# Softmax denominators of the first half's queries: probabilities added on VectorE, one multiplication by ones on TensorE

## What is computed

```python
paths = jax.nn.sigmoid(x @ Wp + bp)             # (8, 1024, 8 heads, 5)
agree = pq * pk + (1.0 - pq) * (1.0 - pk)
sim = jnp.cumprod(agree, axis=-1).sum(axis=-1) / DEPTH
sim = jnp.where(mask[None, None], -jnp.inf, sim)   # causal
attn = jax.nn.softmax(sim, axis=-1)
ctx = jnp.einsum('bhqk,bhkd->bhqd', attn, V)
x = _layernorm(x + ctx @ Wo)
x = _layernorm(x + w_down(silu(w_gate(x)) * w_up(x)))
```

## Time and profile before

| | |
|---|---|
| median of 3 runs | 944.2 us (944.07 to 945.45) |
| profiled execution | 944.54 us, of which 942.8 us from the first to the last instruction |
| TensorE matmul busy | 846.7 us (90%) |
| VectorE busy | 480.6 us (51%) |
| ScalarE busy | 456.3 us (48%) |
| GpSimd busy | 227.6 us (24%) |
| mean granted TensorE clock | 0.973 of full speed |

### The profile page before, as it was taken

One profiled execution on the slowest core, in us unless ns is written; L12 is line 12 of the kernel. 1 busy time (PEld: TensorE's weight loads), 2 busy tenths in 40 slices (PEclk: granted clock), 3 DMA queues, 4 the chain that ended last, 5 costly groups with the idle time before them and its releaser, 6 DMA issues.

```text
span 942.8 us, 15453 instructions
## 1 busy us (share of the span) xinstructions
PE 846.7 (90%) x6146; PEld 412.6 (44%) x6146; DVE 480.6 (51%) x1021; ACT 456.3 (48%) x721; POOL 227.6 (24%) x266
## 2 busy tenths in 40 slices
PE   5399998899989999799988999899998999898984
PEld 3144355443544436344454435444363444344352
DVE  2844436445465436554275354654355552754375
ACT  2255644546355454554546454555535545364431
POOL 0021231223222232131321223122421313222222
PEclk9599999999999999999999999999999999999997
DMA  6841443140421424104431314214150043200001
GB/s 214 208 105 46 90 90 113 45 88 26 112 90 46 113 45 113 67 23 112 91 112 46 71 43 112 90 46 90 49 132 23 24 113 83 75 2 22 1 1 47
DMA packets 44362, 71.09 MB, mean 75 GB/s; under 512 B 3584, under 2 KB 21248, under 8 KB 44288
## 3 DMA queue, kind: packets, MB, share of 16 engines
q1 hardware_dynamic: 44288, 70.07, 28.4%
HBM read 53.28 MB, written 16.78 MB: 74 GB/s over the span
## 4 chain that ended last, share of the span: by engine, by line
PE 73%; DVE 9%; ACT 8%; issue 3%; DMA 3%; POOL 3%; SPq 1%; POOLq 0%; ACTq 0%; DVEq 0%
PE ctx_ps L788 14%; PE misc L823 12%; PE den_ps L788 12%; PE slot L766 11%; PE misc L833 8%; PE misc L742 7%; ACT probs L451 6%; PE misc L800 6%; POOL work L404 2%; DVE work L612 2%; PE misc L751 2%; DVE x L595 2%; DVE ctx_raw L522 1%; DMA phi_dram<-phi_lo 1%; ACT work L463 1%
## 5 line engine op out<-in xcount | busy, mean ns | idle before, releaser
L451 ACT ACTIVATE probs<-slot 128x1024 f32<-128x1024 f32 (+3 forms) x384 | 290.4, 808 | 374.5 <-PE slot L766 374.2
L766 PE MATMUL slot<-query_stack,key_stack 128*128 128x512 f16 (+3 forms) x768 | 162.8, 334 | 16.6 <-DMA query_stack<-phi_dram 15.4
L788 PE MATMUL ctx_ps<-probs,vz_sb 128*32 128x512 f32 (+3 forms) x1536 | 166.0, 504 | 10.0 <-DVE ctx_raw L522 9.7
L404 POOL TENSOR_TENSOR work<-work 128x512 f16<-128x512 f32 x96 | 112.7, 1174 | 216.5 <-ACT work L469 216.5
L788 PE MATMUL den_ps<-probs,ones 128*32 128x512 f32 (+3 forms) x1536 | 163.0, 496 | 0.0
L390 POOL TENSOR_SCALAR_AFFINE_SELECT probs<-probs 128x512 f32<-128x512 f32 x128 | 81.7, 640 | 309.2 <-ACT probs L451 308.1
L612 DVE SCALAR_TENSOR_TENSOR work<-work,misc 128x512 f32<-128x512 f32 x90 | 61.8, 686 | 165.7 <-ACT work L463 165.7
L823 PE MATMUL misc<-x1T_hi,w_parts 128*128 128x512 f16 x360 | 136.7, 380 | 1.4 <-DVE x1T_lo L602 0.9
L823 PE MATMUL misc<-x1T_lo,w_parts 128*128 128x512 f16 x360 | 136.4, 379 | 0.0
L766 PEld LDWEIGHTS slot<-query_stack,key_stack 128*128 128x128 f16 x768 | 56.9, 98 | 171.2 <-issue 121.7
L833 PE MATMUL misc<-w_parts,work 128*128 128x256 bf16 x720 | 83.7, 273 | 8.3 <-POOL work L404 8.3
(11 more groups left out here) (74 smaller groups left out, 645.3 us busy)
## 6 DMA issues: line engine op xcount, KB each, us to landing
key_stack<-phi_dram SPq DMA_DIRECT2D x64, 256.0 KB, 6.0
query_stack<-phi_dram SPq DMA_DIRECT2D x64, 256.0 KB, 6.6
xT_sb<-in_xT_dram SPq DMA_DIRECT2D x8, 1024.0 KB, 5.1
x_sb<-in_x_dram SPq DMA_DIRECT2D x8, 1024.0 KB, 5.5
out_dram<-x SPq DMA_DIRECT2D x15, 512.0 KB, 2.9
phi_dram<-phi_hi SPq DMA_DIRECT2D x16, 256.0 KB, 2.1
phi_dram<-phi_lo SPq DMA_DIRECT2D x16, 256.0 KB, 2.3
work<-in_wgT_dram SPq DMA_DIRECT2D x1, 768.0 KB, 8.1
```

Source lines behind the costliest of these rows:

```text
L404: pool.tensor_tensor(hid_lo[:, n % M1, :], hid[:, n % HSLOTS, :], hid_hi[:, n % M1, :], ALU.subtract).then_inc(hid_lo_ready, 1)
L451: act.activation(probs[:, s % P_SLOTS, 2 * p:2 * p + 2, off:CH], slot[p][:, :, off:CH], ACT.Exp).then_inc(slot_drained[p], 1)
L766: mm = pe.matmul(slot[p][:, k, off:CH], key_stack[:, h, P * j:P * (j + 1)], query_stack[:, h, CH * c + off:CH * (c + 1)], start=True, stop ...
L788: mm = pe.matmul(sums[32 * k:32 * k + 32, off:CH], w, probs[:, s % P_SLOTS, k, off:CH], start=first, stop=final)
```

## The change

In the short chunks (c=0) the multiplication by ones no longer runs in every step. VectorE gets a new entry `sum` in the list (`add_up`), one step after `exps` and ahead of that step's other work: at j=1 it copies the first 128 columns of step j=0's probabilities into a new tile `acc` and adds the other 384 columns of the two steps; at j=2 and j=3 it adds 256 and 128 columns, for the four heads in one instruction each. In the chunk's last step TensorE multiplies `acc` by ones once, 512 columns wide. ScalarE's `exps`, before it overwrites a slot of `probs` that held a short step, now waits for the sum that read it (for j=0, the sum at j=1) besides `weigh`. `normalise` waits for the multiplication of `acc`. Steps of the second half (c=1) keep their multiplications.

```diff
+    SHORT = [i for i, (q, c, g, j) in enumerate(STEPS) if c == 0]
...
+        if s >= 1 and (s - 1) % NS in SHORT:
+            plan += [("sum", *divmod(s - 1, NS))]
         plan += between(b, i)
...
+        acc = sb("acc", [P, 4, CH], F32)
...
                     act.wait_ge(pv_done, s - P_SLOTS + 1)
+                    b2, i2 = divmod(s - P_SLOTS, NS)
+                    if i2 in SHORT:
+
+                        act.wait_ge(summed, SUMMED[b2, i2 + (STEPS[i2][3] == 0)])
...
+            def add_up(b, i):
+
+                q, c, g, j = STEPS[i]
+                if j == 0:
+                    return
+                s = NS * b + i
+                own = probs[:, s % P_SLOTS, :, P * j:CH]
+                dve.wait_ge(masked, len(DIAG) * b + DIAG.index(i) + 1)
+                if j == 1:
+                    if NG * b + g >= 1:
+                        dve.wait_ge(acc_used, NG * b + g)
+                    first = probs[:, (s - 1) % P_SLOTS, :, :]
+                    dve.tensor_copy(acc[:, :, 0:P], first[:, :, 0:P]).then_inc(summed, 1)
+                    dve.tensor_tensor(acc[:, :, P:CH], first[:, :, P:CH], own, ALU.add).then_inc(summed, 1)
+                else:
+                    dve.wait_ge(summed, SUMMED[b, i] - 1)
+                    dve.tensor_tensor(acc[:, :, P * j:CH], acc[:, :, P * j:CH], own, ALU.add).then_inc(summed, 1)
...
                 dve.wait_ge(pv_done, NS * b + LAST[q] + 1)
+                if c == 0:
+                    dve.wait_ge(acc_used, NG * b + g + 1)
...
-                for sums, taken in ((ctx_ps, ctx_out), (den_ps, den_out)):
-                    if first and NQ * b + q >= 1:
-                        pe.wait_ge(taken, NQ * b + q)
+                if first and NQ * b + q >= 1:
+                    pe.wait_ge(ctx_out, NQ * b + q)
+                for k in range(4):
+                    h = 4 * g + k
+                    mm = pe.matmul(ctx_ps[32 * k:32 * k + 32, off:CH], vz_sb[:, b % 2, j, 32 * h:32 * h + 32],
+                                   probs[:, s % P_SLOTS, k, off:CH], start=first, stop=final)
+                if c == 0:
+
+                    mm.then_inc(pv_done, 1)
+                    if final:
+                        pe.wait_ge(summed, SUMMED[b, i])
+                        if NQ * b + q >= 1:
+                            pe.wait_ge(den_out, NQ * b + q)
+                        for k in range(4):
+                            mm = pe.matmul(den_ps[32 * k:32 * k + 32, :], ones[:, :], acc[:, k, :],
+                                           start=True, stop=True)
+                        mm.then_inc(acc_used, 1)
+                else:
+                    if first:
+                        pe.wait_ge(den_out, NQ * b + q)
                     for k in range(4):
-                        h = 4 * g + k
-                        w = vz_sb[:, b % 2, j, 32 * h:32 * h + 32] if taken is ctx_out else ones[:, :]
-                        mm = pe.matmul(sums[32 * k:32 * k + 32, off:CH], w,
+                        mm = pe.matmul(den_ps[32 * k:32 * k + 32, off:CH], ones[:, :],
                                        probs[:, s % P_SLOTS, k, off:CH], start=first, stop=final)
-                mm.then_inc(pv_done, 1)
+                    mm.then_inc(pv_done, 1)
```

More of the change, by code:

```diff
@@ L180, in seq_postln_kernel @@
             turn += 1
+    SUMMED, pieces = {}, 0
+    for b in range(B):
+        for i in SHORT:
+            pieces += (0, 2, 1, 1)[STEPS[i][3]]
+            SUMMED[b, i] = pieces
     NORM = {tuple(n): at for at, n in enumerate([n for what, *n in PLAN if what == "stats"])}
@@ L275, in seq_postln_kernel @@
         den_out = sem("den_out")
+        summed = sem("summed")
+        acc_used = sem("acc_used")
         den_recip_ready = sem("den_recip_ready")
@@ L697, in _ @@
                     split_weights()
+                elif what == "sum":
+                    add_up(*n)
                 elif what == "normalise":
```

## The result

The changed kernel takes 968.94 us (median of 4 runs, 968.58 to 971.09) against 944.48 us for the kernel before beside it: ratio 1.0238, 95% interval 1.0189 to 1.0287, so 24.5 us slower. The forecast was 961, the range 948 to 974.

The account below looks back on a forecast made before the run. TensorE (90% busy) bound the kernel, with half-idle VectorE nearly as tight in steps 2 to 7 and the bound in step 6. Middle batches +6, batch 0 +6.5, batch 7 +4 on 944.54 gave 961 us, range 948 to 974.

Parts of the forecast that it names:

- The adds: VectorE, each short chunk: copy 0.42 us, adds 1.75, 1.2 and 0.65 us; 4 us a chunk, 64 us in 16 chunks.
- its idle time: TensorE ahead of `turn_f`, step 6 of middle batches: grows from 2.48 to 4.8 us, `turn_f` moving from 271.42 to 272.9.
- batch 0's scores: Scores of step 4 in batch 0: wait for the first copy and add, moving from 54.87 to 58.7, +3.8 us.
- The net of a middle batch at full clock: Middle batches, TensorE savings against VectorE delays with no fall of the clock: +0.9 us a batch.
- that wait, named as a sign: Step 8 of middle batches: gate matmul newly waits for the VectorE instruction behind the second add, 1.3 us late.
- All three terms of the sum: Whole run: middle batches +6 us, batch 0 +6.5 and batch 7 +4, together 16.5 us.
- the last one: Batch 7, with no next batch's work to cover VectorE: +4 us, bounds +1 and +6.
- With idle times twice as long I take a fall of that length in all six: Middle batches, step 6: the clock falls for about 3.3 us in all six, before in three; +6 us in all.
- with one of twice the length some +13: Upper bound for the six middle batches together if the clock's fall lasts twice as long: some +13 us.
- TensorE stays the bound: Rival, whole run: every add lies in VectorE's idle half, the 21 us come in full, 923 us; chance 0.07.
- the 21 us: TensorE's saving from fewer multiplications by ones: 1.32 us a short chunk, 21 us in 16 chunks.
- Dearer adds: Rival: VectorE and GpSimd in each other's way, 0.3 us more per add on the chain, 973 us; chance 0.13.

Follow-up runs that it names:

- experiment 3: Changed kernel plus 20 unread 512-column matmuls in TensorE's step 6 idle time, batches 1 to 6: 957.96 us, ratio 1.0134 to the kernel before.
- experiment 5: Changed kernel with the new way for the first short chunk of a batch alone, the second multiplied by ones every step: 950.2 us, ratio 1.0042.
- experiment 6: Changed kernel with the new way for the second short chunk of a batch alone, the first multiplied by ones every step: 962.61 us, ratio 1.016.
- experiment 2: Changed kernel with adds and copies cut to one column (denominators not computed) and ten unread matmuls in step 6: 937.06 us, ratio 0.9904.
- experiment 8: Changed kernel with second chunk's adds moved behind `x1_low` and the hidden products, second half of weights' split later, 10 unread matmuls: 959.32 us, ratio 1.0125.
- experiment 4: Kernel before the change plus 10 unread 512-column matmuls in step 6 idle time of batches 1 to 6: 940.06 us, ratio 0.9934.
- experiment 10: Changed kernel, new way in batches 1 to 6 alone, adds behind what TensorE waits for, four `probs` slots, 10 unread matmuls: 930.33 us, ratio 0.9836.

## Why the prediction was right, and where its sizes were off

**Right, step by step.** The adds took what was derived: copy 0.42, adds 1.75, 1.21 and 0.69 us (the row that the first was taken from the earlier trace rows reads int32, but the times agree). `turn_f` came at 281.10 - 8.17 = 272.93 (forecast 272.9), its idle time at 4.73 (4.8); batch 0's scores at 58.45 (58.7). The net of a middle batch at full clock, +0.9, was measured as 110.98 - 110.07 = 0.91 (experiment 3), with the wait for L648 that it derives. In the changed kernel itself that wait, named as a sign, did not come: there the lower clock makes TensorE later than L648. The sign came from VectorE's chain, not from its share of 51%, and experiments 5 and 6 bear that out: as many adds cost the run 0.4% in one place and 1.6% in the other. All three terms of the sum came out too small, the last one, 7.3, beyond its bound of 6; that the total still lies in the range is owed to the range's width.

**Mis-sized: the clock.** The sign and the waits were right; the step that was mis-sized is "With idle times twice as long I take a fall of that length in all six". The fall came in all six, but it lasted 6.8 us in five of them. About 2 us of that lie in the idle time itself, the rest over work. Batch 1, the one with a fall of the length taken, stood at 0.0 (0.15 forecast). Batches 2, 4 and 5, whose counterparts before were at full clock, lost 2.3 to 2.5 us instead of 1.8; batches 3 and 6, whose counterparts had a fall, 0.8 and 0.9 instead of 0.15. Together that is 9.1 us instead of 6. The bound "with one of twice the length some +13" is the case that nearly came. The steps shown give some 16 for it, with 3.3 us instead of 1.65 on TensorE; what they leave out is that a part of the low clock falls into the idle time, where TensorE has no work to slow. Experiment 3 gives the clock's part in the middle batches by itself: 8.8 us. Rule and row met here: the Trainium skill's warning against idle gaps (TensorE: Matmul & The Clock Gate, HAM oscillation) named the right mechanism, since the clock fell in all six middle batches and held, at 1.00, where TensorE was kept busy (experiment 3).

**Mis-sized: batch 0 and the end, by the clock too.** Batch 0's wait for the pair cost the 3.6 us foreseen. The fall behind it was taken as 1.6 and lasted 10 us with the idle time in it, so that `normalise` of the first chunk came 6.35 us late (63.53 to 69.88) instead of 5.6; the pair of step 6 then added its 2.0 in full, since no wait swallowed a part of it: the scores of step 8, behind bias, squash and exponential, and `turn_f`, behind the features, both come 8.3 us late. In batch 7 the gate matmul moved from 820.71 to 842.09, 4.1 more than the batch's start had (3.5 forecast); the steps behind it, with a low clock of 3.4 us from there on, added another 1.2. Some 2 us more came in the ending, which has no instruction of the change. The same five microseconds behind the transposes of x1, before and after:

```profile
907.00:912.00 5.00, 4.82 (x38) 3.86 (x39) 2.16 (x4) 1.29 (x3) 0.00 (x0) 1.00 0.00 0
```

```profile
929.60:934.60 5.00, 4.86 (x29) 3.82 (x30) 1.37 (x3) 1.09 (x2) 0.00 (x0) 0.66 0.00 0
```

As much idle time ahead of it, 2.14 us before and 2.13 after, left the clock full before and let it fall after: whether a short idle time does so is not set by its length alone. What else decides was not tried.

**The rivals.** "TensorE stays the bound" was wrong in a second way: even with the adds at one column and the clock full, a batch gains 1.6 of 2.64 us (experiment 2). So the 21 us were not all there to be had: TensorE's busy time falls by 2.19 us a batch, and new waits take a part of that. "Dearer adds" was right in kind and small: the second add of batch 2's second chunk took 1.65 us beside a mask, the first chunk's, with no mask beside it, 1.21; over all 16 of this shape the mean is 1.39.

## What to carry to other kernels

Work moved to an engine that is half idle costs by where it stands in that engine's list: ask which instruction of the bound engine waits for what comes next there, and follow the wait through every in-order list on the way, as experiment 8 shows by failing to. An idle time of the matrix engine can cost twice, once itself and once through a lower clock behind it; where it can't be removed, a few matmuls that nobody reads are worth trying, here 0.7% by themselves. Before judging whether the idea pays, place the added work behind everything that is waited for: the same adds gave +2.4% as written and, placed behind it in six of eight batches, with the busy matmuls (0.7% by themselves) and a fourth slot of `probs`, -1.6%.

## What the hardware showed that was not expected

Behind these waits the low clock lasted 3.4 us after 2.48 us of idle time, in three batches of six; 6.8 us after 4.73, in all five; and 10.2 us in batch 0, where 4.76 us of idle time followed 2.06. The idle time does not settle it alone: after the 4.5 us of experiment 6 it lasted 3.4 us in three batches and 6.8 in three. Unread matmuls in the idle time kept it at 1.00 in every middle batch of experiments 2, 3, 4 and 10; in experiment 8, where another idle time of 2.0 us followed, it fell behind that in four of six.
